# Key stacks filled in four waiting steps, and the feed-forward of a two-layer attention kernel put in other places of its schedule

## The chip, the core and the metric

The kernel runs on one core of one Trainium2 chip. The metric is device time in microseconds (us) of one execution; a version's time is the median of its runs. Engines are named as in the profile: PE (TensorE matmul), PEld (its weight loads), DVE (VectorE), ACT (ScalarE), POOL (GpSimd), SP (SyncE, which here only issues DMAs and waits for them).

## What is computed

64 batch elements of 64 tokens and 128 features go through two layers. Layer 0 is causal self-attention joined with attention to a context, then a feed-forward with two layer norms ahead of it; layer 1 is masked cross-attention to the same context.

```python
qkv = (_ln(x, g1, be1) @ w_qkv + b_qkv).reshape(b, t, 3, h, dh)     # h = 16 heads of dh = 8
ckv = (context @ w_ckv + b_ckv).reshape(b, s, 2, h, dh)
k = concatenate([k_self, k_ctx], axis=1); v = concatenate([v_self, v_ctx], axis=1)
attn = softmax(where(mask, q @ k * scale, -inf))
x = x + attn @ v
hdn = _ln(_ln(x, g2, be2), gf, bf) @ w1 + b1                        # 128 -> 512
x = x + (gelu(hdn) @ w2 + b2)                                       # 512 -> 128
# layer 1
Q = qn @ wq.T + bq; K = context @ wk.T + bk; V = context @ wv.T + bv
probs = softmax(where(key_mask == 0, NEG_INF, Q @ K / sqrt(hd)))
out = (probs @ V) @ wo.T + bo + x
```

## The kernel before

**Chunks, units and slots.** The batch is cut into 8 chunks (c = 0 to 7) of 8 batch elements, 512 tokens. Attention is done in units: eight for a chunk's layer 0, four for its layer 1, 96 in all. Time is counted in slots, and every engine walks through the same slots (`for s in ALL`) with its own list of what is due in each. In slot s PE makes the scores by query of unit s + 3 (`by_query`, tile `query`), the scores by key of unit s + 1 (`by_key`, tile `key`), and the product of probabilities and values of unit s (`values`). In between stand the maxima on DVE (`take_top`, tile `top`, L1011), a split of them on POOL (L462), and the exponentials on ACT (`exp`, tile `probs`, L523), which `by_key` of the next unit and `values` wait for. One chunk takes 12 slots. Chunk c's layer 0 begins in slot 12c, its layer 1 in slot 12c + 32 (a little earlier for the last two). The last thing in a slot is `dense`: one or two of the large products, placed by the table `JOBS` (name, start list, slot relative to the start). They share two PSUM banks in turn, so that each job waits until the one before the last has been read.

**Feed-forward.** For chunk c: in slot 12c + 9 the first norm (DVE), then gain and offset on POOL; in slot 12c + 11 the statistics of the second norm (DVE) and their root (POOL, L455); in slot 12c + 12 the normalisation (DVE, L979); in slot 12c + 13 job `f_t`, four transposes into `normed_ft` (PE L684, read by ACT L564), and at the slot's end `w1_0` and `w1_1`, in slot 12c + 14 `w1_2` and `w1_3` (PE L689, 128x512 each). ACT applies Gelu to the four in one go (L610) at the end of slot 12c + 13. Exp and Gelu lie in different tables of ACT, so a table load stands before the first Gelu, where a Gelu of one column (`unread`, L608) brings it on early, and another before the next exp. Then follow `w2a` and `w2b` (L712). Between these, in slot 12c + 14, PE transposes the context of a later chunk (job `ctx_t`, L684 from `ctx_in`).

**Stacks.** Scores need keys and queries in split form (a high and a low part), stacked over partitions. They are written to DRAM (`scratch_k`, `scratch_q`, L340 and L344) and read back into `k_stack`, `q_stack`, `k1_stack`, `q1_stack`. All of that is on one queue, SP, which issues in order and stands still while it waits. In slot 12c - 17, which is slot 7 of a chunk's twelve, SP issues for chunk c: the key stack (`fill_keys`, two DMAs of 384 KB, L357), a wait until both have landed, the query stack in two steps of two DMAs of 96 KB with a wait between (`fill_queries`, L369), and behind them the load of an x chunk (L392), the stores and the fill of a layer 1 query stack, the load of a context chunk (L419) that `ctx_t` waits for, and in slot 11 the keys of layer 1 (L357, two DMAs of 192 KB, no wait behind). The profile prints `k1_stack` as k_stack and `q1_stack` as q_stack.

**Instructions.** PE runs 8885 matmuls, each with a weight load. Its instructions come in blocks over DMA queue q8, 70 packets of 16 KB in this run.

Of the kernel before, what the change touches and what calls it, by code (L numbers as in the profile page):

```python
# [14 lines left out]
P = 128  # L15
# [21 lines left out]
KEYMASK = 32768.0  # L37
Q_HIGH, Q_LOW = slice(0, 2), slice(2, 3)
# [11 lines left out]
IN = L0  # L50
# [38 lines left out]
JOBS = (("f_t", L0, 13), ("w1_0", L0, 13), ("w1_1", L0, 13), ("w1_2", L0, 14), ("w1_3", L0, 14), ("ctx_t", IN, -22),  # L89
# [56 lines left out]
def xattn_program(nc, io, consts, out):  # L146
    ctx = ExitStack()
    with ctx:
# [28 lines left out]
        unread = sb("unread", [P, CHUNKS])  # L177
# [159 lines left out]
        def _(sp):  # L337
# [41 lines left out]
            for s in ALL:  # L379
                for c in due(-18, s, IN):  # L380
                    if c > 0:
                        sp.wait_ge(s_fill["k"], 32 * c)
# [14 lines left out]
                for c in due(-17, s, IN):  # L397
                    if c > 0:
                        sp.wait_ge(s_fill["q"], 64 * c)
# [9 lines left out]
                    if c > 0:  # L409
                        sp.wait_ge(s_fill["k"], 32 * (c + 1))  # L410
# [9 lines left out]
                for c in due(11, s):  # L420
                    if c > 0:
                        sp.wait_ge(s_fill["k1"], 48 * c)
# [8 lines left out]
                for c in due(22, s, X2):  # L431
                    if c > 0:
                        sp.wait_ge(s_fill["q1"], 64 * c)
# [15 lines left out]
        def _(pool):  # L449
# [23 lines left out]
            for s in ALL:  # L473
# [17 lines left out]
                for c in due(6, s):  # L491
                    pool.wait_ge(s_mask, 16 * (c + 1))
                    if c > 0:
                        pool.wait_ge(s_read["k1"], c)
                        pool.wait_ge(s_fill["k1"], 48 * c)
# [20 lines left out]
                for c in due(11, s):  # L516
                    root(c, "x1_again")

        @block.scalar
        def _(act):  # L520
# [48 lines left out]

            def dense_first(s):  # L570
# [5 lines left out]
            def dense(s):  # L576
# [64 lines left out]
            for s in ALL:  # L641
                if s + 1 in UNIT:
# [26 lines left out]
        def _(pe):  # L669
# [46 lines left out]
            def dense_first(s):  # L716
                for c in job_due("f_t", s):
                    pe.wait_ge(s_norm["x1_again"], c + 1)
                    transposes("f_t", c, normed_f)
                for c in job_due("w1_2", s):  # L720
# [3 lines left out]
            def dense(s):  # L724
# [4 lines left out]
                for c in job_due("w1_0", s):  # L729
# [457 lines left out]
```

## Time and profile before

| what | value |
|---|---|
| runs, median | 465.14 us (3 runs, 463.82 to 467.96) |
| profiled execution | 466.13 us, its span 463.7 us |
| busy PE, DVE, ACT, POOL | 83%, 64%, 57%, 30% of the span |
| granted TensorE clock, mean | 0.915 of full speed |
| DMA queue q1 (SP's) | 39.86 MB, 31.2% of 16 engines |
| chain that ended last | PE 50%, DVE 18%, issue 9%, ACT 8%, DMA 8%, POOL 4% |

Times within the trace are us from the span's start. "Issue" in the chain is time in which an engine waited for nothing that the profile shows. The clock column PEclk is 1.00 at full speed; 0.50 is half of it.

### The profile page before, as it was taken

The page shows a single profiled execution, that of the slowest core. Times are in us where ns is not written, and L with a number is a line of the kernel's source. Part 1 is how long each engine was busy: PE and PEld are TensorE (multiplying, and loading weights), DVE is VectorE, ACT ScalarE, POOL GpSimd, SP SyncE. Part 2 cuts the span into 40 slices and gives each one's busy share as a digit, 9 for nine tenths or more (in the row PEclk, how much of TensorE's full clock was granted, in tenths as well). Part 3 has the DMA queues.
Part 4 walks back from the last instruction along what each step waited for, and adds up shares of the span by engine and source line. Part 5 has one row for each costly group of instructions (what it writes and reads, how often), then busy time and mean ns, then how long its engine had stood idle before and what let it go on. Part 6 is the DMA issues. An engine that isn't in the chain of part 4 may idle for free.

```text
span 463.7 us, 20194 instructions
## 1 busy us (share of the span) xinstructions
PE 384.7 (83%) x8885; PEld 278.6 (60%) x8885; DVE 295.5 (64%) x738; ACT 262.5 (57%) x459; POOL 139.8 (30%) x207
## 2 busy tenths in 40 slices
PE   3668879996989799988899798979898989686766
PEld 1346657564666576657576567667676676453654
DVE  5426786469568774796658675796389459706232
ACT  2567635763756476464846386556656756343451
POOL 7100533046205520363105520461047106302000
PEclk9957986999999899998999899998999999877586
DMA  6755164115342542153404542253201400121101
GB/s 192 198 151 123 54 171 140 34 56 137 108 119 93 121 147 59 69 129 111 134 3 146 106 131 60 94 122 122 60 26 43 125 3 26 58 82 47 48 4 45
DMA packets 41974, 42.86 MB, mean 92 GB/s; under 512 B 3208, under 2 KB 34392, under 8 KB 41888
## 3 DMA queue, kind: packets, MB, share of 16 engines
q1 hardware_dynamic: 40436, 39.86, 31.2%
q8 instruction: 70, 1.15, 1.1%
q0 software_dynamic: 624, 1.26, 1.0%
q10 hardware_dynamic: 828, 0.46, 0.3%
q14 instruction: 16, 0.13, 0.1%
HBM read 23.65 MB, written 17.83 MB: 89 GB/s over the span
## 4 chain that ended last, share of the span: by engine, by line
PE 50%; DVE 18%; issue 9%; ACT 8%; DMA 8%; POOL 4%; SPq 1%; ACTq 1%; DVEq 0%; POOLq 0%
PE dense L689 12%; PE dense L712 7%; DVE top L1011 5%; PE key L845 3%; PE mixed L875 3%; PE mixed L883 3%; DMA k_stack<-scratch_k 3%; PE key L836 3%; PE side L908 3%; PE dense L694 3%; PE dense L702 2%; PE query L795 2%; PE query L803 2%; DVE k_part L1001 2%; ACT probs L523 2%
## 5 line engine op out<-in xcount | busy, mean ns | idle before, releaser
L1011 DVE TENSOR_REDUCE top<-query 128x8 f32<-128x1024 f32 (+1 forms) x96 | 117.2, 1220 | 70.9 <-PE query L803 54.7
L523 ACT ACTIVATE probs<-key 128x1024 f32<-128x1024 f32 x96 | 98.4, 1025 | 81.9 <-PE key L845 55.7
L462 POOL TENSOR_TENSOR top<-top 128x8 bf16<-128x8 f32 (+1 forms) x96 | 20.3, 213 | 207.2 <-DVE top L1011 206.5
L845 PE MATMUL key<-top_row,spread 48*64 48x128 bf16 x1536 | 48.7, 226 | 3.8 <-ACT top_row L528 3.6
L455 POOL TENSOR_TENSOR rstd_x<-var_eps_x,half 128x4 f32<-128x4 f32 x24 | 24.5, 1020 | 71.6 <-DVE var_eps_x L973 71.6
L544 ACT COPY o_t<-mixed 128x256 f32<-128x256 f32 x96 | 35.3, 368 | 13.4 <-PE mixed L896 7.8
L875 PE MATMUL mixed<-probs,v 128*32 128x128 f32 x1024 | 41.7, 281 | 0.0
L836 PE MATMUL key<-q_stack,k_stack 48*64 48x128 f16 x1024 | 40.1, 221 | 0.0
L689 PE MATMUL dense<-normed_ft,w 128*128 128x512 f32 x64 | 34.2, 663 | 5.1 <-ACT normed_ft L564 5.1
L845 PEld LDWEIGHTS key<-top_row,spread 48*64 48x64 bf16 x1536 | 33.8, 109 | 6.1 <-ACT probs L523 4.9
L908 PE MATMUL side<-cst,o_t 128*128 128x128 f32 x192 | 34.1, 304 | 0.7 <-ACT mix_t L551 0.7
L712 PE MATMUL dense<-w,hidden 128*128 128x128 f32 x256 | 31.9, 278 | 2.8 <-DVE x L1044 2.2
L712 PEld LDWEIGHTS dense<-w,hidden 128*128 128x128 f32 x256 | 29.7, 192 | 4.6 <-DVE x L1044 3.4
L883 PE MATMUL mixed<-probs,v 128*32 128x64 f32 x1024 | 25.5, 241 | 8.3 <-issue 7.9
L836 PEld LDWEIGHTS key<-q_stack,k_stack 48*64 48x64 f16 x1024 | 31.8, 109 | 0.1
L875 PEld LDWEIGHTS mixed<-probs,v 128*32 128x32 f32 x1024 | 24.3, 110 | 12.5 <-issue 8.2
L829 PE MATMUL key<-hide_query,own_keys 64*64 64x512 bf16 x128 | 25.5, 395 | 7.0 <-ACT probs L523 6.9
L528 ACT COPY top_row<-mixed 128x128 bf16<-128x128 bf16 x96 | 26.9, 280 | 6.6 <-PE mixed L896 6.6
L702 PE MATMUL dense<-w_qkv,normed_t 128*64 128x128 f32 x128 | 23.0, 338 | 6.6 <-DVE k_full L1111 2.3
L610 ACT ACTIVATE hidden<-dense,cols 128x512 f32<-128x512 f32 x32 | 21.1, 682 | 12.1 <-PE dense L689 12.1
L908 PEld LDWEIGHTS side<-cst,o_t 128*128 128x128 f32 x192 | 22.2, 150 | 8.5 <-issue 6.9
L896 PE MATMUL mixed<-identity_b,top 128*32 128x128 bf16 x192 | 23.5, 229 | 3.8 <-POOL top L462 3.8
(120 smaller groups left out, 782.1 us busy)
## 6 DMA issues: line engine op xcount, KB each, us to landing
k_stack<-scratch_k SPq DMA_DIRECT2D x16, 384.0 KB, 6.2
q_stack<-scratch_q SPq DMA_DIRECT2D x64, 96.0 KB
scratch_k<-k_part SPq DMA_DIRECT2D x8, 512.0 KB, 2.8
scratch_k<-k_part SPq DMA_DIRECT2D x16, 256.0 KB, 2.6
scratch_q<-q_part SPq DMA_DIRECT2D x16, 256.0 KB, 2.7
k_stack<-scratch_k SPq DMA_DIRECT2D x16, 192.0 KB
x_in<-in_x SPq DMA_DIRECT2D x8, 256.0 KB, 3.2
scratch_q<-q_part SPq DMA_DIRECT2D x16, 128.0 KB, 2.4
```

Source lines behind the costliest of these rows:

```text
L523: nc.scalar.activation(probs[u.number % 2][:].rearrange("p h q -> p (h q)"), key[:].rearrange("p h x -> p (h x)"), ACT.Exp, scale=SCALE).t ...
L528: nc.scalar.copy(top_row[u.number % 2][:], turned).then_inc(s_row, 1)
L544: nc.scalar.copy(dst, src).then_inc(s_o_t, 1)
L689: nc.tensor.matmul(b[:], w, src[:], start=True, stop=True).then_inc(s_done[name], 1)
L702: nc.tensor.matmul(b[0:T, n * D:(n + 1) * D], normed_t[:, at], w_qkv[:, 2 * D:3 * D], start=True, stop=True)
L712: ins = nc.tensor.matmul(b[:, n * D:(n + 1) * D], hidden[:, f, n * P:(n + 1) * P], w2[:, f, :], start=(f == 0), stop=(f == FC - 1))
L836: nc.tensor.matmul(key[T * n:T * n + T, h, a * P:(a + 1) * P], k_stack[c % 2][rows, a, b, T * n:T * n + T], q_stack[c % 2][rows, a, :, b * ...
L845: ins = nc.tensor.matmul(key[T * n:T * n + T, h, a * P:(a + 1) * P], spread[u.layer][rows, A2 * h + a, T * n:T * n + T], top_row[u.number ...
L875: ins = nc.tensor.matmul(mixed[32 * j:32 * j + 32, P * a:P * a + P], v0[c % 2][:, b, 2 * p:2 * p + 2].rearrange("p s w -> p (s w)"), pr[:, ...
L883: ins = nc.tensor.matmul(mixed[32 * j:32 * j + 32, T * g:T * g + T], v1[c % 2][:, b, h].rearrange("p s w -> p (s w)"), pr[:, at, :], start ...
L908: ins = nc.tensor.transpose(side[:, n * P:(n + 1) * P], o_t[s // 2 % 2 - 1][:, n].rearrange("p b q -> p (b q)"), identity)
L1011: nc.vector.tensor_reduce(maxima, query[:].rearrange("p h x -> p (h x)").rearrange("p (a k) -> p a k", a=w), AX_X, ALU.max, negate=True).t ...
```

## The change

Two things are changed.

The key stacks (`fill_keys`, both layers) are filled by eight DMAs in place of two, in four steps of two; from chunk 1 on SP waits before each further step until the step before has landed. The counts that others wait for follow in a table `FILLS`. For chunk 0 the eight are issued in a row.

The second norm of the feed-forward and `f_t` come a slot sooner: statistics and root in slot 12c + 10, normalisation in slot 12c + 11, `f_t` in slot 12c + 12. The four w1 products stay in their slots, but stand between the slot's scores by query and its scores by key (`up`) instead of at the end of slot 13 and behind the scores by key of slot 14. ACT does Gelu 0 and 1 at the end of slot 13, and 2 and 3 at the start of slot 14, ahead of the exponential; the one-column Gelu remains for the last chunk alone.

```diff
+FILLS = {"k": 32 * A2, "q": 64, "k1": 32 * A2 + 16, "q1": 64}
-JOBS = (("f_t", L0, 13), ("w1_0", L0, 13), ("w1_1", L0, 13), ("w1_2", L0, 14), ("w1_3", L0, 14), ("ctx_t", IN, -22),
+JOBS = (("f_t", L0, 12), ("w1_0", L0, 13), ("w1_1", L0, 13), ("w1_2", L0, 14), ("w1_3", L0, 14), ("ctx_t", IN, -22),
...
             def fill_keys(name, c, stack, first):
                 sp.wait_ge(s_store[name], 32 * (c + 1))
-                for h in range(HALVES):
-                    at = HR * h + first
-                    sp.dma_start(stack[at:at + ROWS], rows_of(name, h)).then_inc(s_fill[name], 16)
+                for a in range(A2):
+                    if a > 0 and c > 0:
+                        sp.wait_ge(s_fill[name], FILLS[name] * c + FILLS[name] - 32 * (A2 - a))
+                    for h in range(HALVES):
+                        at = HR * h + first
+                        sp.dma_start(stack[at:at + ROWS, a:a + 1], rows_of(name, h)[:, a:a + 1]).then_inc(s_fill[name], 16)
...
-                for c in due(11, s):
+                for c in due(10, s):
                     root(c, "x1_again")
...
+            def gelu(c, f):
+                nc.scalar.activation(hidden[:, f, :], job(f"w1_{f}", c)[:], ACT.Gelu,
+                                     bias=cols[:, B1 + f:B1 + f + 1]).then_inc(s_read[f"w1_{f}"], 1)
...
-                for c in job_due("w1_1", s):
+                for c in job_due("w1_0", s):
                     if c > 0:
                         act.wait_ge(s_done["w2b"], c)
-                    act.wait_ge(s_half, 1)
-                    nc.scalar.activation(unread[:, c:c + 1], half[:, 0:1], ACT.Gelu)
-                    for f in range(FC):
-                        nc.scalar.activation(hidden[:, f, :], job(f"w1_{f}", c)[:], ACT.Gelu,
-                                             bias=cols[:, B1 + f:B1 + f + 1]).then_inc(s_read[f"w1_{f}"], 1)
+                    if c == LAST:
+                        act.wait_ge(s_half, 1)
+                        nc.scalar.activation(unread[:], half[:, 0:1], ACT.Gelu)
+                    gelu(c, 0)
+                    gelu(c, 1)
...
             for s in ALL:
+                for c in job_due("w1_2", s):
+                    gelu(c, 2)
+                    gelu(c, 3)
                 if s + 1 in UNIT:
                     exp(UNIT[s + 1])
...
                 if s + 3 in UNIT:
                     by_query(UNIT[s + 3])
+                up(s)
                 if s + 1 in UNIT:
                     by_key(UNIT[s + 1])
...
-                for c in due(12, s):
+                for c in due(11, s):
                     norm_rows(c, "x1_again", normed_f, normed_f)
```

On PE, around slots 13 and 14 of chunk 1's feed-forward, the order before (query is written by `by_query`, key by `by_key`, mixed by `values` and the turned maxima):

```order
L684 MATMUL dense1<-cst,normed_f 128x128 x3
L875 MATMUL mixed<-probs0,v00 32x128 [waits s_row,s_o_t,s_probs]
...
L689 MATMUL dense0<-normed_ft,w1 128x512 [waits s_read_v1,s_read_f_t]
L689 MATMUL dense1<-normed_ft,w1 128x512 [waits s_read_f_t]
...
L803 MATMUL query<-k_stack0,q_stack0 64x128 x16
L829 MATMUL key<-hide_query,own_keys 64x512 [waits s_probs]
...
L845 MATMUL key<-top_row0,spread0 64x128 x15
L689 MATMUL dense0<-normed_ft,w1 128x512 [waits s_read_w1_0]
L689 MATMUL dense1<-normed_ft,w1 128x512 [waits s_read_w1_1]
```

And now, where `f_t` has gone a slot further up:

```order
L818 MATMUL query<-k_stack0,q_stack0 64x128 x16
L702 MATMUL dense0<-normed_ft,w1 128x512 [waits s_read_v1,s_read_f_t]
L702 MATMUL dense1<-normed_ft,w1 128x512 [waits s_read_f_t]
L844 MATMUL key<-hide_query,own_keys 64x512 [waits s_probs]
...
L818 MATMUL query<-k_stack0,q_stack0 64x128 x16
L702 MATMUL dense0<-normed_ft,w1 128x512 [waits s_read_w1_0]
L702 MATMUL dense1<-normed_ft,w1 128x512 [waits s_read_w1_1]
L844 MATMUL key<-hide_query,own_keys 64x512 [waits s_probs]
```

The scores by key of both slots now come behind a pair of w1 products, and the second pair waits for Gelu 0 and 1 with those scores queued behind it.

On ACT the same place before:

```order
L523 ACTIVATE probs1<-key 128x1024 [waits s_scores_k]
L564 ACTIVATE normed_ft<-dense1,cols 128x512 [waits s_done_f_t,s_done_w1_3]
...
L608 ACT_TABLE_LOAD [waits s_half]
L608 ACTIVATE unread<-half 128x1 [waits s_done_w2b]
L610 ACTIVATE hidden<-dense0,cols 128x512 [waits s_done_w1_0]
```

And now:

```order
L529 ACTIVATE probs1<-key 128x1024 [waits s_scores_k]
...
L577 ACT_TABLE_LOAD [waits s_done_w1_0]
L577 ACTIVATE hidden<-dense0,cols 128x512 [waits s_done_w2b]
L577 ACTIVATE hidden<-dense1,cols 128x512 [waits s_done_w1_1]
L577 ACTIVATE hidden<-dense0,cols 128x512 [waits s_done_w1_2]
L577 ACTIVATE hidden<-dense1,cols 128x512 [waits s_done_w1_3]
L529 ACT_TABLE_LOAD
L529 ACTIVATE probs0<-key 128x1024 [waits s_scores_k]
```

The exponential of slot 13 still comes before the table load and the Gelus, and the scores that it reads are now made after the first w1 pair.

On SP, chunk 2's stacks before:

```order
L357 DMA k_stack0<-scratch_k 48x4x1024 [waits s_store_k,s_scores_k]
L357 DMA k_stack0<-scratch_k 48x4x1024
L369 DMA q_stack0<-scratch_q 24x4x512 [waits s_store_q,s_fill_k]
...
L392 DMA x_in0<-in_x 128x4x128 [waits s_x1]
L419 DMA ctx_in1<-in_ctx_1024 128x4x128 [waits s_done_ctx_t]
```

And now:

```order
L363 DMA k_stack0<-scratch_k 48x1024 [waits s_store_k,s_scores_k]
L363 DMA k_stack0<-scratch_k 48x1024
L363 DMA k_stack0<-scratch_k 48x1024 [waits s_fill_k]
L363 DMA k_stack0<-scratch_k 48x1024
L363 DMA k_stack0<-scratch_k 48x1024 [waits s_fill_k]
L363 DMA k_stack0<-scratch_k 48x1024
L363 DMA k_stack0<-scratch_k 48x1024 [waits s_fill_k]
L363 DMA k_stack0<-scratch_k 48x1024
L375 DMA q_stack0<-scratch_q 24x4x512 [waits s_store_q,s_fill_k]
```

Three waits more stand ahead of the query stack, the x load and the context load.

## Rows read from the trace of the kernel before

**Rows 1.** The page: the chain that ended last, by engine.

```profile
PE 50%; DVE 18%; issue 9%; ACT 8%; DMA 8%; POOL 4%; SPq 1%; ACTq 1%; DVEq 0%; POOLq 0%
```

**Rows 2.** The chain in order of time: start, length, what.

```profile
156.11 2.53 issue
...
207.07 3.02 issue
...
258.42 3.08 issue
...
310.27 2.04 issue
```

**Rows 3.** Windows: length; busy PE, PEld, DVE, ACT, POOL (x count); PEclk, DMA share, GB/s.

```profile
199.50:207.00 7.50, 6.92 (x242) 5.18 (x229) 7.23 (x16) 5.00 (x10) 3.90 (x6) 1.00 0.66 125
207.00:211.00 4.00, 0.98 (x35) 0.71 (x31) 2.23 (x3) 0.91 (x1) 3.84 (x4) 0.92 0.20 54
211.00:216.00 5.00, 5.00 (x112) 4.14 (x113) 2.35 (x4) 1.44 (x3) 0.20 (x1) 0.72 0.54 174
```

**Rows 4.** The DMA view of 200 to 209, in 40 slices of 0.225 us.

```profile
DMA  0000039300925699999999999999621130000000
```

**Rows 5.** The DMA view of 207.0 to 207.5: the instruction queue.

```profile
q8 instruction: 1, 0.02, 16.8%
```

**Rows 6.** SP's timeline during chunk 5's and chunk 6's fills.

```profile
200.84 1.25 SPq L357 DMA_DIRECT2D k_stack<-scratch_k  x2
208.36 3.44 SPq L369 DMA_DIRECT2D q_stack<-scratch_q  x4
...
220.22 0.39 SPq L419 DMA_DIRECT2D ctx_in<-in_ctx  x1
...
251.96 1.76 SPq L357 DMA_DIRECT2D k_stack<-scratch_k  x2
260.26 4.10 SPq L369 DMA_DIRECT2D q_stack<-scratch_q  x4
...
273.57 0.40 SPq L419 DMA_DIRECT2D ctx_in<-in_ctx  x1
```

**Rows 7.** The page's DMA issues: size, us to landing.

```profile
ctx_in<-in_ctx SPq DMA_DIRECT2D x7, 256.0 KB, 3.5
```

**Rows 8.** SP's timeline during chunk 3's fill.

```profile
106.47 0.88 SPq L357 DMA_DIRECT2D k_stack<-scratch_k  x2
113.45 3.37 SPq L369 DMA_DIRECT2D q_stack<-scratch_q  x4
```

**Rows 9.** The timeline at 129, PE: in brackets the idle time before and its releaser.

```profile
129.21 0.66 PE L684 MATMUL dense<-cst,ctx_in 128*128 128x128 f32 x4 [1.22 <-DMA ctx_in<-in_ctx]
```

**Rows 10.** The timeline of 33 to 48, SP and DVE.

```profile
33.55 1.04 SPq L357 DMA_DIRECT2D k_stack<-scratch_k  x2
40.24 3.90 SPq L369 DMA_DIRECT2D q_stack<-scratch_q  x4
...
47.15 0.88 DVE L967 BATCH_NORM_STATS2 stat_x<-x_in 128x6 f32<-128x128 f32 x4 [2.05 <-DMA x_in<-in_x]
```

**Rows 11.** The timeline of 220 to 230, PE and ACT.

```profile
220.32 0.66 PE L684 MATMUL dense<-cst,normed_f 128*128 128x128 f32 x4
...
222.19 1.98 PE L689 MATMUL dense<-normed_ft,w 128*128 128x512 f32 x4 [0.59 <-ACT normed_ft L564]
...
227.25 0.69 ACT L610 ACTIVATE hidden<-dense,cols 128x512 f32<-128x512 f32 x1 [0.17 <-PE dense L689]
...
227.95 1.28 ACT L523 ACT_TABLE_LOAD   x1
...
229.25 1.02 ACT L523 ACTIVATE probs<-key 128x1024 f32<-128x1024 f32 x1
```

**Rows 12.** The page's groups: ACT's two copies of each unit.

```profile
L544 ACT COPY o_t<-mixed 128x256 f32<-128x256 f32 x96 | 35.3, 368 | 13.4 <-PE mixed L896 7.8
L528 ACT COPY top_row<-mixed 128x128 bf16<-128x128 bf16 x96 | 26.9, 280 | 6.6 <-PE mixed L896 6.6
```

More of the change, by code:

```diff
@@ L176, in xattn_program @@
         half = sb("half", [P, TILES])
-        unread = sb("unread", [P, CHUNKS])
+        unread = sb("unread", [P, 1])
         cst = sb("cst", [P, CW])
@@ L381, in _ @@
                     if c > 0:
-                        sp.wait_ge(s_fill["k"], 32 * c)
+                        sp.wait_ge(s_fill["k"], FILLS["k"] * c)
                     sp.wait_ge(s_high["k_ctx"], c + 1)
@@ L398, in _ @@
                     if c > 0:
-                        sp.wait_ge(s_fill["q"], 64 * c)
+                        sp.wait_ge(s_fill["q"], FILLS["q"] * c)
                     store_high("q", c, Q_HIGH, twice(q_part[:, 0]))
@@ L409, in _ @@
                     if c > 0:
-                        sp.wait_ge(s_fill["k"], 32 * (c + 1))
+                        sp.wait_ge(s_fill["k"], FILLS["k"] * (c + 1))
                     fill_queries("q", c, q_stack[c % 2], 0, c > 0)
@@ L421, in _ @@
                     if c > 0:
-                        sp.wait_ge(s_fill["k1"], 48 * c)
+                        sp.wait_ge(s_fill["k1"], FILLS["k1"] * c)
                     if c >= 2:
@@ L432, in _ @@
                     if c > 0:
-                        sp.wait_ge(s_fill["q1"], 64 * c)
+                        sp.wait_ge(s_fill["q1"], FILLS["q1"] * c)
                     store_high("q1", c, Q_HIGH, twice(q1_part[:, 0]))
@@ L494, in _ @@
                         pool.wait_ge(s_read["k1"], c)
-                        pool.wait_ge(s_fill["k1"], 48 * c)
+                        pool.wait_ge(s_fill["k1"], FILLS["k1"] * c)
                     nc.gpsimd.tensor_scalar(keep[:], mask_in[:], 0, 0, ALU.is_equal, ALU.is_equal).then_inc(s_keep, 1)
@@ L719, in dense_first, with up @@
                     transposes("f_t", c, normed_f)
+            def up(s):
+                for c in job_due("w1_0", s):
+                    pe.wait_ge(s_read["f_t"], c + 1)
+                    product("w1_0", c, w1[:, 0:P], normed_ft)
+                    product("w1_1", c, w1[:, P:2 * P], normed_ft)
                 for c in job_due("w1_2", s):
@@ L728, in dense @@
                     to_features(s)
-                for c in job_due("w1_0", s):
-                    pe.wait_ge(s_read["f_t"], c + 1)
-                    product("w1_0", c, w1[:, 0:P], normed_ft)
-                    product("w1_1", c, w1[:, P:2 * P], normed_ft)
                 for c in job_due("ctx_t", s):
@@ L782, in by_query @@
                     if u.layer == 0:
-                        pe.wait_ge(s_fill["k"], 32 * (c + 1))
-                        pe.wait_ge(s_fill["q"], 64 * (c + 1))
-                    else:
-                        pe.wait_ge(s_fill["k1"], 48 * (c + 1))
-                        pe.wait_ge(s_fill["q1"], 64 * (c + 1))
+                        pe.wait_ge(s_fill["k"], FILLS["k"] * (c + 1))
+                        pe.wait_ge(s_fill["q"], FILLS["q"] * (c + 1))
+                    else:
+                        pe.wait_ge(s_fill["k1"], FILLS["k1"] * (c + 1))
+                        pe.wait_ge(s_fill["q1"], FILLS["q1"] * (c + 1))
                         pe.wait_ge(s_mask_keys, 32)
@@ L1071, in statistics @@
                     stats("x", x_in[c % 3], range(TILES))
-                for c in due(11, s):
+                for c in due(10, s):
                     dve.wait_ge(s_offset, c + 1)
```

## The prediction

> **What bounds the kernel now.** The page first: the chain that ended last runs half over PE, with 9% in "issue" [rows 1]. The chain in order of time shows where that is. Four pieces of 2.0 to 3.1 us stand each in the middle of a unit's `values`, where no semaphore is waited for [rows 2]. All four lie at the end of a key stack's fill, those of chunks 4 to 7. The windows between PE's instruction packets say why [rows 3]. A block carries about 127 matmuls with their weight loads (8885 over 70 packets), and the window from 211 to 216 has 112. The one that covers chunk 5's fill has 242, and the next has 35: PE ran through two blocks before a packet came, and then stood. The DMA engines are full from 203 to 206.5 [rows 4] and the packet is seen at 207.0 [rows 5], some 3.5 us after the block was used up. So a fill of 768 KB in one go holds up PE's own instructions. The reader is to see also what follows: the granted clock, 1.00 up to 207, is 0.72 on average from 211 to 216 [rows 3], because it falls to half after the idle 3 us.
>
> The second thing that ends last is SP's queue. Chunk 3's fill goes out at 106.47, and PE waits 1.22 us for the context load behind it [rows 8, 9]. At the start DVE waits 2.05 us for the x load behind chunk 1's fill [rows 10]. In chunks 4 to 6 the queue is hidden, since those stretches are the long ones with the stall in them.
>
> **The fill in four steps, what it removes.** Each step has 192 KB, like the two steps of a query stack, and beside those I see no such stall. I take it that the stalls go. Worth: chunk 5's 3.02 us, and the half clock behind it, which costs about 1.2 us; DVE then has its own backlog, so I count 3.4 us and not 4.2 up to the slot of `f_t`.
>
> **What it adds.** A step is two issues and a landing. The nearest rows are the query fills, of equal bytes: four DMAs with one wait between take 3.37, 3.44, 3.90 and 4.10 us [rows 6, 8, 10]; less about 0.75 for the last two issues, a step is 2.6 to 3.35, on average 2.95. From the other side: 768 KB in one go took 6.98 us [rows 8] and 192 KB 2.6, so 192 KB more cost 1.45 and most of a step is fixed. I take 2.8, near the low end since the queues are otherwise empty in the middle of a fill, and keep 2.6 and 3.2. Four steps are 11.2 us (10.4 to 12.8), against 6.7 for chunk 1 (40.24 less 33.55), 7.0 for chunk 3, 7.5 for chunk 5 and 8.3 for chunk 6 [rows 6, 8, 10]. So all that is queued on SP behind a fill comes 3 to 4.5 us later. For each place I ask what is late next.
>
> Start (chunk 1): the x load was already waited for; DVE's statistics, and the maxima and PE's scores behind them in order, come 4.5 us later. **+4.5.** Chunk 3: PE already waited for the context; +4.2, and an idle time of over 4 us should bring the half clock after it, +0.8. **+5.0.**
>
> Chunk 5: the context load goes out at 220.22 and takes 3.5 [rows 6, 7], so it lands at 223.7, now at 227.4. With its transposes (0.6) and the next scores by query (0.5), the scores by key of slot 15 begin at 228.5; before they began at 230.3, when the exponential ended [rows 11]. The stall's end would allow 227.7; the queue gives it at 228.5. **-1.8**, and the same for chunk 4, -1.8. Chunk 6: its load goes out at 273.57, lands at 277.1, now 2.9 later at 280.0, and with 1.1 behind it 281.1 against 281.4 (chunk 5's 230.3 and one period of 51.1). **-0.3.** Chunk 7 has no context load behind it: 2.04 us and about 0.9 of clock go, less the feed-forward's cost below. **-1.6.** The keys of layer 1 hold SP through four steps as well, but only the mask's load stands behind them until the next chunk. Chunk 0's eight DMAs cost SP six more issues, well ahead of PE's first scores: 0.
>
> At one place the Trainium skill gives another sum. "DMA: Bandwidth & Descriptors", in the section "Anatomy of one DMA — SWDGE (gpsimd) path", fits a DMA of the other issuing path as 2.0 us and bytes over 436 GB/s: 2.45 a step and 9.8 a fill, by which the total would be about 466 instead of 471. The rows here (2.6 at the best) are slower, and I go by them.
>
> **The feed-forward.** The norm a slot sooner costs DVE and POOL nothing that I count: DVE stands idle in slot 10 before the next maxima, as PE is then in its stall or just out of it, and the offset is ready. `f_t` moves 0.6 us of PE from slot 13 to slot 12, and PE's wait of 0.59 for its reading goes [rows 11]. But the scores by key of slot 13, which ended at 220.32, now come behind 0.6 of `f_t` and 2.0 of w1, at 223.0 [rows 11]. From there ACT is a line: exponential 1.02, two copies 0.65 [rows 12], table load 1.28, Gelu 0.69: 226.6. Before, the load ran beside the first w1 pair. The second pair waits for that Gelu with the scores by key behind it: PE stands 2.6 us, and ends at 228.6; Gelu 3 0.69, the load for the exponential 1.28, the exponential 1.02: 231.65 against 230.3. **+1.35** for each chunk where nothing else ends later. That is within the bound of chunks 4 to 6 (the queue), and counted in chunk 7; in the stretch of chunk 2's fill it is +1.35 less about 0.85 of clock, **+0.5**; in the feed-forward of chunk 6, which has no fill beside it, **+1.35**; in the last chunk no units stand around it, 0. The bounds: 0 if Gelus and scores interleave better than in this line, 2.6 if all of PE's wait is lost.
>
> **Sum.** +4.5 +5.0 +0.5 -1.8 -1.8 -0.3 -1.6 +1.35 = +5.85, on the profiled execution 466.13 + 5.85 = 472.0. That execution lies 0.2% above the median shown, 465.14, and on that scale the forecast is **471.0 us**, 1.3% slower. A change of under 1% is about what a measurement of this kernel can't tell from none.
>
> **Rivals.** *A step is short, and the kernel faster.* Place: SP's queue behind the fill. If with 192 KB in flight the engines move rows as fast as they move x (two to three times the fill's rate in one go), a step could be 1.9 us and a fill 7.5: start +0.8, chunk 3 +0.6, chunk 2 +0.5, chunks 4 to 6 -2.6 each by the exponential, then -1.6 and +1.35, together -6.15: 459. It decides from the step on: below 2.5 us the sum is negative, below about 2.0 faster by over 1%. For it: the fill in one go is slow for its bytes. Against it: no query step was under 2.6. 14%.
>
> *The feed-forward costs nothing.* Then chunks 2, 6 and 7 give back 1.35 each, 4.05 in all, and the queue still holds: 467. 20%.
>
> *Steps of 3.2 us*, since the fixed part is paid four times beside other loads: 1.6 more at five places, of which one had slack: 478. 17%.
>
> *The stalls stay, and the change doesn't do what it says.* The window counts could also be had if PE's packets were late for a reason of their own. Then the five places behind a fill keep their stall, with +1.35 each, and the start and chunk 3 as above: 466.13 + 9.5 + 8.1, or 482.7 on the median's scale. Against it: the counts double at fills alone. 6%. The Trainium skill has a rule of this kind: "DMA: Bandwidth & Descriptors", "Queues, rings and completion order", says that each engine goes round its queues by packets, so that a queue of PE's own should not wait for a whole fill. The trace disagrees: 242 matmuls passed before a packet came.
>
> **How the numbers follow.** The forecast's own case (468 to 475) holds 43%. The range takes in the short steps' upper part and the long ones: 461 to 477, which leaves out the stalls that stay, the fastest of the short steps and the slowest of the long. Faster by over 1% needs short steps: 0.15. Within 1% (460.5 to 469.8) come the free feed-forward, a step of 2.6 and the rest of the short steps: 0.38. Slower: 0.47.
>
> **What would show it.** In the changed kernel's chain the pieces of "issue" in `values` at fills are gone, and windows between packets hold about 127 matmuls; else the stalls stay. From a fill's first issue on SP to the first query DMA 11.2 us: 10.4 or 12.8 move the total by some 4 us. PE's transposes of the context wait for the load in chunks 3 to 6, by over 4 us in chunk 3, and DVE's statistics at the start by 6.5. In slot 14 PE idles about 2.6 us before the second w1 pair. I am wrong if the SP queue turns out not to be waited for behind the first fill and chunk 3's, or if steps are under 2.5 us.

## The result, and the profile after

The changed kernel takes **481.24 us** (median of 4 runs, 478.85 to 482.47), the kernel before 464.48 beside it: a ratio of 1.035, 95% interval 1.027 to 1.043. The forecast was 471.0 with a range of 461 to 477: slower, as forecast, but by 16.8 us and not 6. Medians here are of all runs of a kernel; ratios and intervals leave out runs more than 1.5% above its fastest. The profiled execution took 480.41 us, its span 478.5; before, the span was 463.7.

The page's chain by engine, where DMA was 8% and PE 50% [rows 1]:

```profile
PE 37%; DMA 20%; DVE 18%; ACT 8%; issue 8%; POOL 6%; SPq 3%; ACTq 1%; DVEq 0%; POOLq 0%
```

**The stalls are gone.** The windows between PE's instruction packets around chunk 5's fill (columns as in [rows 3]):

```profile
206.25:210.00 3.75, 3.75 (x150) 2.24 (x148) 3.58 (x11) 2.14 (x4) 3.05 (x4) 1.00 0.65 214
210.00:214.75 4.75, 4.18 (x154) 3.51 (x144) 4.49 (x10) 3.07 (x6) 2.24 (x3) 1.00 0.26 75
214.75:219.25 4.50, 4.50 (x126) 3.09 (x114) 4.50 (x8) 3.27 (x7) 3.65 (x5) 1.00 0.30 87
```

Where one window had 242 matmuls and the next 35 [rows 3], there are now 150, 154 and 126, at the full clock. Of the chain's pieces of "issue" at fills none is over 0.9 us, where four were of 2 to 3 us [rows 2].

**SP's queue is what ends last instead.** Its timeline from chunk 5's fill on, beside [rows 6]:

```profile
210.98 11.04 SPq L363 DMA_DIRECT2D k_stack<-scratch_k  x8
224.88 4.08 SPq L375 DMA_DIRECT2D q_stack<-scratch_q  x4
229.01 0.40 SPq L398 DMA_DIRECT2D x_in<-in_x  x1
...
233.74 3.33 SPq L375 DMA_DIRECT2D q_stack<-scratch_q  x4
237.11 1.66 SPq L425 DMA_DIRECT2D ctx_in<-in_ctx  x1
```

and the chain in order of time there:

```profile
211.43 2.24 DMA k_stack<-scratch_k
214.03 3.20 DMA k_stack<-scratch_k
217.59 3.64 DMA k_stack<-scratch_k
221.59 3.27 DMA k_stack<-scratch_k
225.23 2.43 DMA q_stack<-scratch_q
230.00 3.64 DMA scratch_q<-q_part
234.10 2.24 DMA q_stack<-scratch_q
237.11 4.01 DMA ctx_in<-in_ctx
```

The fill takes 13.90 us up to the query stack (210.98 to 224.88), where it took 7.52 [rows 6]. From the fill's issue to the context's landing it is 30.1 us; before, 22.9 (200.84 to 223.7). PE then stands:

```profile
241.16 0.67 PE L697 MATMUL dense<-cst,ctx_in 128*128 128x128 f32 x4 [4.14 <-DMA ctx_in<-in_ctx]
```

The view of waits (engine, line, releaser: us in total, times, longest) has three that cost. Of the 10.8 us for the context, 3.80 are at the start, the rest in chunks 3, 5 and 6:

```profile
DVE stat_x L984 <- DMA x_in<-in_x: 22.8, 7, 5.6
...
PE dense L702 <- ACT hidden L577: 17.4, 7, 2.5
...
PE dense L697 <- DMA ctx_in<-in_ctx: 10.8, 4, 4.1
```

**The feed-forward.** Chunk 6's, which has no fill beside it, in the timeline:

```profile
378.96 1.02 ACT L529 ACTIVATE probs<-key 128x1024 f32<-128x1024 f32 x1 [2.72 <-PE key L860]
380.43 1.28 ACT L577 ACT_TABLE_LOAD   x1
381.73 1.27 ACT L577 ACTIVATE hidden<-dense,cols 128x512 f32<-128x512 f32 x2
382.47 3.78 PE L702 MATMUL dense<-normed_ft,w 128*128 128x512 f32 x4 [2.49 <-ACT hidden L577]
```

and the window over it:

```profile
382.00:384.00 2.00, 1.53 (x2) 0.84 (x3) 0.00 (x0) 1.00 (x2) 0.00 (x0) 0.50 0.20 49
```

PE idles 2.49 us for Gelu 0, and then the clock is at its lower level (1.2 GHz): the pair that took 1.98 us [rows 11] takes 3.78.

**Where the 14.8 us of span lie**, with the issue of SP's key fills as milestones, and from fill 7 on two of its stores of layer-1 queries:

| stretch | before | after | measured | forecast |
|---|---|---|---|---|
| start to fill 1 | 33.55 | 32.96 | -0.6 | 0 |
| fill 1 to fill 2 (the start) | 29.3 | 35.2 | +6.0 | +4.5 |
| to fill 3 (chunk 2) | 43.6 | 45.1 | +1.4 | +0.5 |
| to fill 4 (chunk 3) | 43.8 | 47.7 | +3.9 | +5.0 |
| to fill 5 (chunk 4) | 50.6 | 50.1 | -0.5 | -1.8 |
| to fill 6 (chunk 5) | 51.1 | 54.2 | +3.1 | -1.8 |
| to fill 7 (chunk 6) | 51.1 | 49.9 | -1.2 | -0.3 |
| to 353.6, now 365.9 (chunk 7) | 50.5 | 50.8 | +0.4 | -1.6 |
| to 395.9, now 412.1 (feed-forward of 6) | 42.3 | 46.2 | +3.9 | +1.35 |
| to the end | 67.8 | 66.4 | -1.4 | 0 |

### The profile page after: what moved, and what is told of

Same layout as the page of the kernel before. It is cut to its first block, busy times and chain, and to the rows that moved or that the text cites. A ratio compares the mean times of both kernels' runs of the same rounds, so it can differ in the third digit from the quotient of the medians.

```text
span 478.5 us, 20283 instructions
## 1 busy us (share of the span) xinstructions
PE 392.7 (82%) x8885; PEld 280.9 (59%) x8885; DVE 296.0 (62%) x738; ACT 262.5 (55%) x452; POOL 140.0 (29%) x207
## 3 DMA queue, kind: packets, MB, share of 16 engines
q8 instruction: 70, 1.15, 1.0%
## 4 chain that ended last, share of the span: by engine, by line
PE 37%; DMA 20%; DVE 18%; ACT 8%; issue 8%; POOL 6%; SPq 3%; ACTq 1%; DVEq 0%; POOLq 0%
PE dense L702 10%; DMA k_stack<-scratch_k 9%; PE dense L725 6%; DVE top L1028 5%; DMA q_stack<-scratch_q 4%; PE mixed L890 3%; DMA scratch_q<-q_part 2%; PE key L860 2%; DVE k_part L1018 2%; DMA ctx_in<-in_ctx 2%; PE key L851 2%; PE side L923 2%; PE dense L697 2%; ACT probs L529 2%; SPq L375 2%
## 5 line engine op out<-in xcount | busy, mean ns | idle before, releaser
L1028 DVE TENSOR_REDUCE top<-query 128x8 f32<-128x1024 f32 (+1 forms) x96 | 117.1, 1219 | 54.2 <-PE query L818 37.7
L860 PE MATMUL key<-top_row,spread 48*64 48x128 bf16 x1536 | 51.8, 232 | 6.3 <-ACT top_row L534 5.5
L702 PE MATMUL dense<-normed_ft,w 128*128 128x512 f32 x64 | 39.7, 754 | 17.6 <-ACT hidden L577 17.4
L890 PE MATMUL mixed<-probs,v 128*32 128x128 f32 x1024 | 42.9, 287 | 0.0
L851 PE MATMUL key<-q_stack,k_stack 48*64 48x128 f16 x1024 | 42.5, 228 | 0.0
L860 PEld LDWEIGHTS key<-top_row,spread 48*64 48x64 bf16 x1536 | 36.2, 112 | 9.0 <-ACT probs L529 5.4
L851 PEld LDWEIGHTS key<-q_stack,k_stack 48*64 48x64 f16 x1024 | 33.4, 114 | 0.3
L702 PEld LDWEIGHTS dense<-normed_ft,w 128*128 128x128 f32 x64 | 13.2, 228 | 31.3 <-ACT hidden L577 22.6
L534 ACT COPY top_row<-mixed 128x128 bf16<-128x128 bf16 x96 | 26.8, 280 | 5.5 <-PE mixed L911 5.5
L1040 DVE RECIPROCAL rden<-side 128x16 f32<-128x16 f32 x32 | 8.0, 251 | 34.2 <-PE side L923 34.2
L844 PE MATMUL key<-hide_query,own_keys 64*64 64x512 bf16 x128 | 26.9, 417 | 1.4 <-ACT probs L529 1.4
L818 PE MATMUL query<-k_stack,q_stack 48*64 48x128 f16 x1024 | 27.0, 224 | 0.0
```

The source lines that it names most:

```text
L534: nc.scalar.copy(top_row[u.number % 2][:], turned).then_inc(s_row, 1)
L702: nc.tensor.matmul(b[:], w, src[:], start=True, stop=True).then_inc(s_done[name], 1)
L818: ins = nc.tensor.matmul(query[T * n:T * n + T, h, a * P:(a + 1) * P], q_stack[c % 2][rows, a, n, b * T:(b + 1) * T], k_stack[c % 2][rows, ...
L844: nc.tensor.matmul(key[0:T, h].rearrange("p (a x) -> p a x", a=A2), own_keys[rows], hide_query[rows].rearrange("p s q -> p (s q)").unsquee ...
L851: nc.tensor.matmul(key[T * n:T * n + T, h, a * P:(a + 1) * P], k_stack[c % 2][rows, a, b, T * n:T * n + T], q_stack[c % 2][rows, a, :, b * ...
L860: ins = nc.tensor.matmul(key[T * n:T * n + T, h, a * P:(a + 1) * P], spread[u.layer][rows, A2 * h + a, T * n:T * n + T], top_row[u.number ...
```

## The experiments

The kernel before ran beside each group, with medians of 461.1 to 462.2; ratios are to it. "FF" is the feed-forward's part of the change.

**1. The two parts apart, and the waits.** Four kernels. `fill_only` is the kernel before with the change's `fill_keys`; `ff_only` is the changed kernel with `fill_keys` of before.

> The kernel before with the fills of both key stacks in four waiting steps, and the feed-forward left where it was. Theory Q (SP's queue behind the longer fills is what ends last): a fill takes 11 to 14 us on SP instead of 6.7 to 8.3, the x load and the context load behind it are waited for in each chunk, and the stalls in values are gone; the start costs +5 to +6, chunk 3 +4, the chunks with stalls win 2 to 3 us each but chunk 5 less: 466 to 474 us, so +2 to +9. Theory F (the feed-forward's new places cost most of the 16.8 us, through PE's wait for the second pair and the half clock behind it): at most +3, 467 or less.

> The changed kernel with the fills as before (two DMAs, no wait between them); the feed-forward's norm, transposes and w1 products in their new places. Theory F: each of the seven feed-forwards with units around it costs 1.35 us of order and some 2.5 us of half clock behind PE's idle time, as chunk 6's did (+3.9 in the changed kernel): +20 to +27, 485 to 491 us, less where a stall lies beside. Theory Q: the order alone, 1.35 us a chunk and no more, +5 to +9.5, 470 to 474 us. In both the four stalls of 2 to 3 us in values at the fills' ends stay.

The third is `fill_only` without the waits between steps:

```diff
-                    if a > 0 and c > 0:
+                    if False:
```

> The kernel before with each key stack filled by eight DMAs issued in a row, without any wait between steps. If it is the bytes in flight that hold up PE's instructions, the four stalls of 2 to 3 us stay and the time is that of before within 1%, 462 to 468 us. If it was the form of the two large DMAs (384 KB each), the stalls go, and as SP is free again after 3.5 us of issue and the landing comes no later, the kernel gains about 10 us: 452 to 457 us.

The fourth is `fill_only` with the x and context loads taken from SP's list and put at the end of ACT's slot:

```diff
-                        sp.dma_start(x_in[c % 3][:], x_d[c]).then_inc(s_x_in[c % 3], 16)
...
-                        sp.dma_start(ctx_in[c % 2][:], ctx_d[c]).then_inc(s_ctx_in[c % 2], 16)
+                        nc.scalar.dma_start(x_in[c % 3][:], x_d[c]).then_inc(s_x_in[c % 3], 16)
...
+                        nc.scalar.dma_start(ctx_in[c % 2][:], ctx_d[c]).then_inc(s_ctx_in[c % 2], 16)
```

> The kernel before with the fills in four waiting steps, and with the loads of x and context chunks from chunk 2 on issued by ACT in the same slots instead of by SP, so that they no longer queue behind a fill. Theory Q: the waits for x and context go, at the start, in chunk 3 and in chunks 4 to 6, while the stalls stay away: 3 to 3.5 us less for each of chunks 4 to 6, 2 to 3 for chunk 7, 2 to 3 for the waits of 2.05 and 1.22 that before had; less 0.4 us of ACT's time for each of 12 issues: 450 to 456 us. If the longer fills cost by the traffic itself or by the stacks' own lateness, it stays at 464 or above.

Measured: `fill_only` **488.5** (1.057, 1.050 to 1.065), `ff_only` **476.2** (1.029, 1.022 to 1.036), eight DMAs in a row **446.4** (0.969, 0.963 to 0.974), waiting steps with the loads on ACT **452.0** (0.983, 0.975 to 0.991). No expectation for `fill_only` reached its size (466 to 474), `ff_only` lies above theory Q's range and below theory F's, and eight in a row came out better than the 452 to 457 expected; the fourth fits theory Q. What costs is plain: the same eight DMAs are 42 us cheaper without their waits, and with the waits 36 of them come back once the two loads don't stand behind them. SP's timeline of the kernel with eight in a row, and its windows between packets:

```profile
198.42 5.48 SPq L363 DMA_DIRECT2D k_stack<-scratch_k  x8
205.62 3.89 SPq L375 DMA_DIRECT2D q_stack<-scratch_q  x4
```

```profile
197.50:202.25 4.75, 4.18 (x152) 3.56 (x144) 4.48 (x10) 3.12 (x6) 2.25 (x3) 1.00 0.45 140
202.25:206.25 4.00, 3.72 (x108) 2.33 (x98) 4.00 (x8) 3.33 (x7) 3.16 (x5) 1.00 0.25 71
```

The fill takes 7.2 us, like the two large ones, and a packet comes in the middle of it: no stall, and no step to pay. The waits buy nothing. (Moving the two loads to ACT is worth nothing by itself: experiment 6 has it without waits, 446.7 against 446.8. So the 36 us are the queue behind the waits.)

Why does `fill_only` lose so much more than 4 us a fill? Its windows and its timeline at chunk 3's context:

```profile
136.00:140.40 4.40, 0.00 (x0) 0.00 (x0) 1.31 (x5) 2.23 (x4) 0.00 (x0) 0.88 0.55 176
140.40:146.40 6.00, 5.99 (x85) 5.07 (x86) 2.25 (x5) 2.15 (x4) 0.24 (x1) 0.52 0.19 50
```

```profile
140.41 1.12 PE L690 MATMUL dense<-cst,ctx_in 128*128 128x128 f32 x4 [4.45 <-DMA ctx_in<-in_ctx]
```

PE waits 4.45 us for the load and then works 6 us at a clock of 0.52. In chunks 3 to 6 it waits so, 4.45 to 5.78 us each (26.0 us in all, with 5.98 at the start). And the delay doesn't end there: the context's transposes lead, some slots on, to the key and query products, whose stores stand ahead of the next fill on SP. The chain that ended last runs the whole way round in `fill_only`: chunk 5's four steps (from 216.86), the query fills, the context load, PE's transposes, and at its end the queries' part on DVE and the next fill.

```profile
242.67 2.87 DMA ctx_in<-in_ctx
245.58 1.11 PE dense L690 x4
...
271.04 1.34 SPq L363
```

So the fill, the query fills, the context load and the next fill hang on each other in a ring, and each fill's extra time (6.3 to 8.1 us in chunks 4 to 7, beside eight in a row) lengthens the period itself: from fill to fill 52.8, 54.2 and 54.5 us in chunks 4 to 6, against 48.9, 46.8 and 47.4 with eight in a row.

**2. The size of a DMA.** Four of 192 KB in a row, with the feed-forward of before:

```diff
-                for a in range(A2):
+                for a in range(0, A2, 2):
...
-                        sp.dma_start(stack[at:at + ROWS, a:a + 1], rows_of(name, h)[:, a:a + 1]).then_inc(s_fill[name], 16)
+                        sp.dma_start(stack[at:at + ROWS, a:a + 2], rows_of(name, h)[:, a:a + 2]).then_inc(s_fill[name], 16)
```

> The kernel before with its key stacks filled by four DMAs of 192 KB in a row, no wait between. Two DMAs of 384 KB gave 461 and the stalls, eight of 96 KB gave 446.4 and none. Theory P (SP's own issue time, 0.7 us a DMA, spreads the bytes, so that an instruction packet comes between them): four are issued in about 2.5 us, most of the fill is in flight at once, and the packet is late by some 2 us of the 3.5: 452 to 458. Rival S (only the size of one DMA matters, and 192 KB is small enough): 446 to 449. Rival F (it is the bytes in flight): 460 to 463.

Measured **453.4** (0.986, 0.972 to 1.000), between the two and within theory P's range. A part of the stall is left, in the chain and in the windows:

```profile
200.29 1.58 issue
```

```profile
193.25:198.75 5.50, 4.92 (x146) 3.77 (x146) 5.23 (x11) 3.98 (x8) 2.99 (x4) 1.00 0.73 159
198.75:203.25 4.50, 2.92 (x95) 2.07 (x96) 3.80 (x8) 2.46 (x6) 3.65 (x5) 1.00 0.24 65
```

Stall at chunk 5: 3.0 us with 2 DMAs, 1.6 with 4, under 1 with 8; 768 KB each time, issued by SP within 1.25, 2.06 and 5.48 us. So it isn't the size of the fill alone. Whether the size of one DMA or the pace of their issue decides can't be told apart by these, since both change together.

**3. The feed-forward's part, with nothing else in the way.** On eight DMAs in a row (446.4), first the whole part, then the second norm and `f_t` alone (their four slot numbers one less), then the whole part with the second w1 pair back behind `by_key`:

> The changed kernel without the waits between the steps of a key stack (eight DMAs in a row). Beside the kernel with eight DMAs in a row and the feed-forward of before (446.4 us) it prices the feed-forward's part with SP's queue short and no stall. Theory C (the price is PE's wait of 2.5 us for Gelu 0 in slot 14 and the half clock behind it): of the 12 us that the feed-forward alone cost, 3.3 are a half clock at the start, where no feed-forward stands; 9 to 10 are left: 456 us (453 to 460). Rival H (the feed-forward's part only costs where a stall or a late load stands beside it): within 2 us of 446.4.

> Eight DMAs in a row, and of the feed-forward's part only the second norm and f_t a slot sooner; the w1 products and the Gelus stay as before. Theory C: the norm and f_t are not the price: 446.4 us, give or take 2. Rival N (the norm in slot 10 and 11 holds up DVE and POOL ahead of the maxima): 451 us or more.

> The kernel with eight DMAs in a row and the whole feed-forward's part, but the second w1 pair behind the slot's scores by key, where it stood before. Theory C: 0.6 us of PE's scores stand in the wait for Gelu 0 and the exponential behind is ready sooner; what is left of the wait (about 1.9) is under what brings the clock down: 449 to 452 us. If the pair's place costs nothing: the same as with the whole part, about 456.

Measured **466.9** (1.012, 1.001 to 1.023), **446.8** (0.962, 0.953 to 0.972) and **462.0** (1.001, 0.996 to 1.006). The sooner norm is free and worth nothing, as expected. The w1 pairs cost 20 us, twice what theory C gave (453 to 460 for the whole part), and the second pair's place is only 5 of them, where 449 to 452 was expected: with the pair moved back PE still waits 1.58 us for Gelu 0 in each of seven chunks, and this pair has the full clock in six of them. Chunk 3's stretch, PE's w1 pairs and ACT, with the norm and `f_t` alone:

```profile
163.89 1.02 ACT L529 ACTIVATE probs<-key 128x1024 f32<-128x1024 f32 x1 [1.08 <-PE key L851]
164.39 1.98 PE L695 MATMUL dense<-normed_ft,w 128*128 128x512 f32 x4
165.37 1.28 ACT L614 ACT_TABLE_LOAD   x1
...
167.49 1.98 PE L695 MATMUL dense<-normed_ft,w 128*128 128x512 f32 x4
...
171.52 1.02 ACT L529 ACTIVATE probs<-key 128x1024 f32<-128x1024 f32 x1
```

and with the whole part:

```profile
168.40 1.98 PE L702 MATMUL dense<-normed_ft,w 128*128 128x512 f32 x4
171.22 1.02 ACT L529 ACTIVATE probs<-key 128x1024 f32<-128x1024 f32 x1 [3.12 <-PE key L860]
172.70 1.28 ACT L577 ACT_TABLE_LOAD   x1
...
174.74 3.24 PE L702 MATMUL dense<-normed_ft,w 128*128 128x512 f32 x4 [2.48 <-ACT hidden L577]
...
180.01 1.02 ACT L529 ACTIVATE probs<-key 128x1024 f32<-128x1024 f32 x1
```

Before, the exponential and the table load run while PE works on the first pair, and the second pair finds its bank read. Now the exponential's scores come behind that pair, ACT idles 3.12 us, and the whole line of exponential, load and Gelu stands between the two pairs. From `f_t` (160.88 and 166.18) to the exponential of slot 14 it is 10.6 us with the norm alone and 13.8 with all.

**4. How much of that is the clock.** PE is given matmuls that nobody reads in the time in which it would wait for Gelu 0, 15 of them and then 10, into the bank of the scores by key, which the slot's scores then overwrite:

```diff
                 for c in job_due("w1_2", s):
+                    if s + 1 in UNIT:
+                        pe.wait_ge(s_probs, UNIT[s + 1].number - 1)
+                    for n in range(15 if s + 1 in UNIT else 0):
+                        nc.tensor.matmul(key[:, 0, 0:P], identity, w1[:, 0:P], start=True, stop=True)
                     product("w1_2", c, w1[:, 2 * P:3 * P], normed_ft)
```

> Eight DMAs in a row and the whole feed-forward's part (466.9 us without the filler), and 15 matmuls (128x128, f32, into the bank of the scores by key, which the slot's scores then overwrite) ahead of the second w1 pair, so that PE is busy in the 2.5 us in which it waited for Gelu 0. The exponential and the Gelus keep their order. Theory C: the clock stays up, the pair takes 2.0 instead of 3.2 us and the scores behind it 0.5 less, seven or eight times: 12 us less, 455 (451 to 459). Rival W (all of the price is PE's wait itself): 465 to 468, or more where the filler ends after the Gelu.

> As the filler of 15 matmuls ahead of the second w1 pair, but with 10 (2.4 us). The 15 took 3.6 us and ended 1.1 us after the Gelu, with the clock up in all seven chunks, and the time was 466.5, as without them (466.9). Theory C (the clock's share is about 1.1 us a chunk, which the late end of the filler ate): 7 to 8 us less, 459 (456 to 462). Rival W (the clock costs nothing there, PE's wait all): 465 to 468.

Measured **466.5** (1.014, 1.008 to 1.020) with 15 and **459.6** (0.998, 0.995 to 1.001) with 10. The rows of the 15 (the profile has each as two records):

```profile
175.43 3.62 PE L743 MATMUL key<-w,cst 128*128 128x128 f32 x30
...
178.88 1.88 PE L702 MATMUL dense<-normed_ft,w 128*128 128x512 f32 x4
```

and of the 10:

```profile
172.79 2.50 PE L743 MATMUL key<-w,cst 128*128 128x128 f32 x20
...
175.22 1.98 PE L702 MATMUL dense<-normed_ft,w 128*128 128x512 f32 x4
```

In both the second pair has the full clock in each of the seven chunks; without a filler it took 1.98 us in two chunks and 2.56 to 3.78 in five. The 15 end late: the pair starts at 178.88, and Gelu 0 was done by 177.8 (two Gelus of 0.63 from 177.12). That takes back what the clock gave. By itself the 466.5 is what rival W expected; the 10, which end in time, decide for theory C (456 to 462 expected): work that nobody needs makes the kernel 7.3 us faster. So of the 20 us, 7 are the clock behind the idle 2.5 us. The other 13 stay with the clock up: from `f_t` (166.66) to the exponential of slot 14 (179.25) it is 12.6 us there, 2.0 more than with the norm alone, and seven times 2.0 is 14. In `ff_only` too the clock is down behind only two of the seven waits, and the part costs 14.0.

**5. Why the whole change is faster than its fill alone.** The medians, by the form of the fill (rows) and the feed-forward:

| key fill | FF as before | FF changed | FF costs |
|---|---|---|---|
| two DMAs | 462.2 | 476.2 | +14.0 |
| eight in a row | 446.4 | 466.9 | +20.5 |
| eight, waiting steps, loads on ACT | 452.0 | 466.0 | +14.0 |
| eight, waiting steps | 488.5 | 481.2 | -7.3 |

The change itself (481.2) ran beside a kernel before of 464.5, not 462.2; by the two ratios (1.057 and 1.035) the last row's difference is some 10 us and not 7.3. Its neighbour above, 466.0, is the change with the loads on ACT:

> The changed kernel with the loads of x and of the context issued by ACT's queue instead of SP's. Theory Q (the waiting steps cost only by what is queued on SP behind them): as without the waits (466.9), and the 5.6 us more that the same move left with the feed-forward of before: 467 to 474. Rival (the steps cost by more than the queue): 477 or more.

Measured 466.0 (1.011, 1.002 to 1.020), a little under the 467 to 474 expected: in the changed kernel the waiting steps cost nothing that shows (466.9 without them) once the loads don't stand behind them. With the feed-forward as before, 5.6 us of them are left (452.0 against 446.4); why these go, no run shows.

Is it the sooner norm that makes the last row negative?

> The kernel before with the waiting steps, and of the feed-forward's part only the second norm and f_t a slot sooner; the w1 products stay. The waiting steps alone gave 488.5, with the whole feed-forward's part 481.2, though that part costs 20 us where nothing waits. Theory E (a late x load holds DVE's statistics, and with the norm ahead of it the feed-forward gets away from it): 481 us or less. Rival O (the w1 products ahead of the scores give it back): 486 to 490.

Measured **483.8** (1.052, 1.041 to 1.064), between the two, and within its own interval (10 us wide) the same as `fill_only`; in its profiled execution the waits for the context are 26.8 us, as in `fill_only` (26.0). In the changed kernel they are 10.8, since the feed-forward's wait stands ahead of them in the same slots and takes their place; and PE's idle time is split in two. At chunk 3 it is 2.49 us for the Gelu, a pair at the lower clock (3.47 us, which costs nothing there, since the load isn't in yet), and 1.56 us for the load; behind that the clock is up:

```profile
139.86 0.66 PE L697 MATMUL dense<-cst,ctx_in 128*128 128x128 f32 x4 [1.56 <-DMA ctx_in<-in_ctx]
```

```profile
140.00:146.00 6.00, 6.00 (x147) 4.82 (x147) 2.64 (x6) 2.73 (x5) 0.24 (x1) 1.00 0.20 56
```

147 matmuls in six us, where `fill_only` did 85. In the six us behind the four context loads of chunks 3 to 6 the clock is 1.00, 1.00, 0.72 and 1.00, and in `fill_only` 0.50 to 0.54 at all four. But of the 7.6 us of span between the two (486.1 and 478.5), 2.8 lie ahead of chunk 2's fill (issued at 71.00 and 68.20), where no feed-forward has begun. To test the clock as the reason, `fill_only` with PE kept busy ahead of its wait for the context, in chunks 3 to 7:

```diff
+                    b = open_job("ctx_t", c)
+                    for n in range(14 if c >= 3 else 0):
+                        nc.tensor.matmul(b[:, 0:P], identity, w1[:, 0:P], start=True, stop=True)
                     pe.wait_ge(s_ctx_in[c % 2], 16 * (c // 2 + 1))
...
```

> The kernel before with the waiting steps (488.5 us), and 14 matmuls (128x128, f32, some 3.4 us, into the bank that the transposes then overwrite) on PE ahead of its wait for the context load, in chunks 3 to 7. PE there waited 4.5 to 6 us and then ran at the half clock for 6 to 8 us; in the changed kernel the feed-forward splits that idle time (2.5 us for the Gelu, then 1.3 to 1.6 for the load) and the clock stays up. Theory K (that is why the whole change is 7 us faster than its waiting steps alone): the clock stays up, 3 us less at each of five places: 473 us (468 to 478). Rival (SP's queue alone sets these stretches, whatever PE's clock): 486 to 490.

Measured **479.8** (1.042, 1.036 to 1.049): 8.7 us less, with no work taken away, though neither the 468 to 478 of theory K nor the 486 to 490 of its rival. That is about as much as the feed-forward's part gives back. But the trace doesn't show that the clock is what gave it. The profiled execution was the slowest of the four (485.4, span 483.5); 2.3 us of its 2.6 us less lie ahead of chunk 2's fill, where no filler runs; and the filler brings the clock up behind one of the four waits, partly behind a second, and not behind the other two, here the first and the third:

```profile
141.00:147.00 6.00, 6.00 (x143) 4.82 (x145) 2.53 (x6) 2.73 (x5) 0.24 (x1) 1.00 0.24 64
247.20:253.20 6.00, 5.95 (x85) 5.03 (x86) 2.25 (x5) 2.63 (x5) 0.24 (x1) 0.51 0.19 54
```

So why the change is faster than its fill alone stays open: the clock behind the context loads is a part that its trace bears out, how large a part isn't shown.

**6. The version that the runs point to**: eight DMAs in a row, norm and `f_t` a slot sooner, loads on ACT.

> The candidate for the fastest: eight DMAs in a row, the second norm and f_t a slot sooner, and the loads of x and of the context on ACT's queue. With the first two 446.8 us. What is left for the third is DVE's wait for x at the start (2.5 us) and the half clock behind it where there is one, against ACT's own issue time (0.5 us, fourteen times): 442 to 447 us.

Measured **446.7** (0.971, 0.966 to 0.977). It is within the 442 to 447 expected, but no better than eight DMAs in a row alone, which is the one edit that is worth having: 3.1% faster than before, and by the two ratios 6.4% faster than the change.

## Why the prediction was wrong

**Right**: what the stall was, that it goes (the rival in which it stays is out), and that SP's queue is what comes next. PE's transposes wait for the context in chunks 3, 5 and 6, though not in 4, and by 1.6, 4.1 and 1.3 us, not by over 4 in chunk 3; DVE's statistics at the start wait 5.6 us (forecast 6.5), and PE 2.5 us for Gelu 0 (2.6). The start, chunk 2 and chunk 3 came to +11.3 together, against +10.0.

**The step's price (2.8 us) was too low**, and by the prediction's own arithmetic (7 us more at 3.2) that is the term that cost most. From a fill's issue to the first query DMA it was 11.2, 12.8, 11.0, 13.4, 13.9, 12.1 and 13.6 us in chunks 1 to 7: 3.1 a step on average, up to 3.5, when PE's stretch is full of other loads. "Near the low end since the queues are otherwise empty" holds for chunks 1 and 3 alone. The estimate worked out from the Trainium skill, 2.45 a step, is further off; the same page ("DMA: Bandwidth & Descriptors", "Anatomy of one DMA — SWDGE (gpsimd) path") says that most of a transfer's fixed time is waiting for its completion, and with that the runs agree: eight DMAs that don't wait take 7.2 us, with three waits 13.9. The prediction's own rows said something else than it read from them: with 2.6 us for 192 KB and 1.45 for each 192 KB more, 1.15 of a step is fixed, which is not most of it.

**The term of chunk 5 (-1.8) had the wrong sign for this reason.** It compared the context's way (228.5) with the old end of the exponential (230.3), and 1.8 us of slack was less than the error of the four steps: the load landed 30.1 us after the fill's issue and not 26.6 (2.7 of the 3.5 are the fill), and it was +3.1. And I compared two moments at one place, where experiment 1 shows a ring in which the longer fill is paid again in each chunk. (The stall's bound of 227.7 there isn't derived; 230.3 less 3.4 and plus 1.35 is 228.25, still under the queue's 228.5, so the sum doesn't change.) Chunks 4 and 7 missed in the same direction, by 1.3 and 2.0.

**The feed-forward's +1.35 was mis-sized.** The line on ACT was the right mechanism. Where no queue hides it, it measured +2.0 between `f_t` and the exponential with the clock up (12.6 us with the 10 fillers, against 10.6) and +3.2 with it down. I had left out that PE's idle 2.6 us can bring the half clock, though I had priced it for longer idle times: of the seven waits of 2.5 us the changed kernel has it behind four; in chunk 6's feed-forward it was +3.9. The rival "costs nothing" is out: without a queue the part costs 14 to 20 us. That it is counted at only three places was right in kind: behind late loads it is hidden, and more than hidden.

**The rivals**: the steps of 3.2 us (478) were the nearest, at 17%; with the feed-forward's clock added at chunk 6's place (+3.9 for +1.35) they reach the measured time (478 + 2.5 = 480.5). The two should have been combined, and the range have gone up to there. That is a sum, and no run gives each term its share.

**What nothing in the prediction saw**: that the waits are not needed. "A fill of 768 KB in one go holds up PE's own instructions" is true of two DMAs of 384 KB, and not of eight of 96 KB in one go. The rule of packets that the prediction cited from the Trainium skill ("DMA: Bandwidth & Descriptors", "Queues, rings and completion order"), against which the two large DMAs speak, fits the eight small ones.

**One reading was off.** The block wasn't used up 3.5 us before the packet came: PE worked until 207.07, the packet crosses at about 207.3, and PE goes on at 210.09. At each of the four stalls PE goes on 2.4 to 3.2 us after the packet, and what passes in between isn't in the trace. That the packet was late, and PE stood for it, holds.

## What to carry to other kernels

Before making a queue wait between pieces of a transfer, try the pieces without the wait: here the split alone took the stall away and 3.1% of the time, and the waits turned that into a loss of 5.7%. A wait on a queue that carries other loads is priced by the longest loop through that queue, not by the slack at one place. And a wait of TensorE can cost twice. Its clock was down (0.50 to 0.54 over six us) behind all four of `fill_only`'s waits of 4.45 to 5.78 us, and behind five (eight DMAs in a row with the whole feed-forward's part), four (the change) and two (`ff_only`) of the seven waits of 2.5 us; behind the seven of 1.58 us (second pair moved back), once. In the changed kernel without the waits of its fill, filling the 2.5 us with matmuls that nobody reads was cheaper than leaving them idle, so long as the filler ended before the wait did.

## What the runs showed of the hardware

- PE's instruction packets are held up by a fill of two DMAs of 384 KB (242 matmuls pass before one comes, and PE stands 3.0 us), half as long by four of 192 KB (1.6 us), not noticeably by eight of 96 KB. "Runtime: NRT & Kernel Launch" of the Trainium skill, "Instruction fetch mechanics", has the fetch hidden behind the issue of instructions; the kernel before shows that it isn't always.
- Matmuls that nobody reads, on PE in its idle time, made two kernels faster, by 7.3 of 466.9 us and 8.7 of 488.5. In the first the clock behind the wait went up with them in all seven chunks; in the second at one place fully.
- The same code's start, which no edit of `ff_only` touches, took 34.4 us from fill to fill and not 29.3. PE idled 2.12 and 1.22 us there, against 0.24 and 1.00 before, and its next products ran at half speed (2.08 us; 1.13 before):

```profile
48.69 0.66 PE L692 MATMUL dense<-cst,ctx_in 128*128 128x128 f32 x4 [2.12 <-DMA ctx_in<-in_ctx]
50.56 0.43 PE L805 MATMUL query<-hide_key,eye_query 64*64 64x256 bf16 x4 [1.22 <-DVE top L1023]
...
53.73 2.08 PE L697 MATMUL dense<-ctx_t,w_ckv 128*128 128x512 f32 x2
```
